# An adaLN block with a gated scan and a top-2 expert layer: GpSimd's row scatters spread over later turns

## What is computed

```python
x = L0_attn_x                                  # (32, 256, 128): 8192 tokens
h = layernorm(x) * (1 + ca) + sa               # ca, sa, ga, ... from silu(c) @ wmod
g = sigmoid(h @ Wg.T + bg); a = sigmoid(h @ Wd.T + bd); v = h @ Wv.T + bv
x = x + ga * (scan(h_t = a_t * h_{t-1} + (1 - a_t) * v_t) * g)
h = layernorm(x) * (1 + cb) + sb
probs = softmax(h @ gate_w.T + gate_b)         # 8 experts
topk_vals, topk_idx = top_k(probs, 2)
y_e = relu(h @ w1_e + b1_e) @ w2_e + b2_e      # hidden width 512
x = x + gb * sum over the two chosen experts of gate * y_e
```

## Time and profile before the change

| | |
|---|---|
| median of three executions | 471.75 us (471.03 to 472.77) |
| span of the profiled execution | 489.7 us |
| the same, over the median | 17.9 us |
| PE, DVE, ACT, POOL busy | 83%, 85%, 61%, 43% of the span |
| attention and routing, up to about | 213 us |
| FFN loop, from there on | 277 us |
| row scatters by GpSimd (L562) | 64, between 92.3 and 212.9 us |

### The profile page before, as it was taken

How to read it: one execution, slowest core, us unless ns; L and a number is a source line. 1 busy time by engine, 2 the same in 40 slices (tenths; PEclk the granted TensorE clock), 3 DMA queues, 4 the chain that set the end, 5 groups by cost and what they waited for, 6 DMA issues and landing times.

```text
span 489.7 us, 14521 instructions
## 1 busy us (share of the span) xinstructions
PE 407.1 (83%) x4122; PEld 337.3 (69%) x4123; DVE 417.7 (85%) x1159; ACT 297.8 (61%) x746; POOL 210.0 (43%) x225
## 2 busy tenths in 40 slices
PE   1959898877887472479999999999999999999960
PEld 1534546445555361359998999999999988998860
DVE  4989889949879759769999899999999999999980
ACT  1536888858787340156676676676676667666640
POOL 7023230683775554833333344444344333433451
PEclk9977889797889555599999999999999999999995
DMA  7624533452331332532333333333323332222220
GB/s 227 169 63 165 162 115 108 173 197 81 116 130 67 114 131 82 168 109 84 91 91 90 79 87 82 89 90 97 85 81 85 82 85 78 71 76 77 67 66 14
DMA packets 47259, 50.51 MB, mean 103 GB/s; under 512 B 5343, under 2 KB 40880, under 8 KB 47203
## 3 DMA queue, kind: packets, MB, share of 16 engines
q1 hardware_dynamic: 39152, 32.64, 24.3%
q0 software_dynamic: 6976, 16.93, 9.4%
q10 hardware_dynamic: 1074, 0.23, 0.2%
HBM read 26.90 MB, written 24.57 MB: 105 GB/s over the span
## 4 chain that ended last, share of the span: by engine, by line
PE 59%; DVE 11%; POOL 10%; issue 9%; SPq 5%; DMA 2%; ACT 2%; POOLq 0%; ACTq 0%; DVEq 0%
PE bank L1500 8%; PE bank L1498 8%; PE bank L1515 8%; PE bank L1518 8%; PE bank L1516 8%; PE bank L1499 8%; POOL sorted_rows L562 8%; PE bank L1364 4%; SPq L422 3%; PE bank L1510 2%; PE bank L1484 2%; DVE st L856 1%; POOL rstd L549 1%; PE bank L1370 1%; DMA xs<-in_L_attn_x_dram 1%
## 5 line engine op out<-in xcount | busy, mean ns | idle before, releaser
L588 POOL DMA_INDIRECT out_dram<-tg,midx x90 | 104.5, 1161 | 163.1 <-DVE tg L1293 149.0
L752 ACT ACTIVATE xs<-bank,b1col 128x256 f32<-128x256 f32 x360 | 136.6, 492 | 21.9 <-PE bank L1500 19.9
L1516 PE MATMUL bank<-w2hi,w2f 128*128 x720 | 119.0, 219 | 1.0 <-issue 1.0
L1515 PE MATMUL bank<-w2hi,xs 128*128 x720 | 119.2, 219 | 0.0
L1274 DVE TENSOR_TENSOR w2f<-xs 128x1024 f16<-128x1024 f32 x90 | 110.3, 1226 | 3.1
L1498 PE MATMUL bank<-xh,w1hi 128*128 128x256 f16 x360 | 99.4, 276 | 2.8 <-ACT xs L752 2.8
L1499 PE MATMUL bank<-xl,w1hi 128*128 128x256 f16 x360 | 99.2, 276 | 0.0
L1500 PE MATMUL bank<-xh,w1lo 128*128 128x256 f16 x360 | 99.2, 275 | 0.0
L1518 PE MATMUL bank<-w2lo,xs 128*128 x720 | 99.0, 219 | 0.0
L562 POOL DMA_INDIRECT sorted_rows<-pay,idx x64 | 68.0, 1062 | 42.8 <-DVE idx L1071 23.5
L1515 PEld LDWEIGHTS bank<-w2hi,xs 128*128 128x128 f16 x720 | 70.2, 98 | 1.8 <-issue 1.1
(11 more groups left out here) (232 smaller groups left out, 673.5 us busy)
## 6 DMA issues: line engine op xcount, KB each, us to landing
xs<-sorted_rows SPq DMA_DIRECT2D x45, 260.0 KB
sorted_rows<-padt SPq DMA_DIRECT2D x10, 582.0 KB
xs<-sorted_rows SPq DMA_DIRECT2D x45, 128.0 KB
w2f<-in_L_ffn_w_dram SPq DMA_DIRECT2D x4, 512.0 KB, 3.8
xs<-in_L_ffn_w_dram SPq DMA_DIRECT2D x4, 512.0 KB, 4.0
xs<-in_L_attn_x_dram SPq DMA_DIRECT2D x3, 512.0 KB, 8.8
out_dram<-tg,midx POOLq DMA_INDIRECT x90
sorted_rows<-pay,idx POOLq DMA_INDIRECT x64
```

What stands on the lines that cost most here:

```text
L588: pool.indirect_dma_start(out_rows, bass.IndirectOffsetOnAxis(midx[k][:, t:t + 1], 0), yout[k][:, t, :], None, bounds_check=TOK - 1, oob_i ...
L752: ins = act.activation(hf[e][:, cc, :], bank[2 * e + cc // 2][:, (cc % 2) * TW:(cc % 2 + 1) * TW], ACT.Relu, bias=b1col[:, bass.ds(ex[e] * ...
L1515: pe.matmul(o[t], hh[n % 2][e][:, cc, t * P:(t + 1) * P], whi, start=False, stop=False)
L1516: pe.matmul(o[t], hl[n % 2][e][:, cc, t * P:(t + 1) * P], whi, start=False, stop=False)
```

## The change

The table of turns is new, and GpSimd takes two new waits. In the turns 8 to 15 the group ahead of `scales` is scattered only once that same turn's scan on VectorE has made its `r` (the count of `r_ready` is the turn's number plus one), and what stands behind `scales` only once that turn's residual is written (`x1_ready`). `scatter` itself, its own waits and the last four groups are as before.

```diff
-SCATTER_IN = {7: ((), (0,)), 8: ((1, 2), ()), 10: ((3, 4), ()), 11: ((), (5,)), 12: ((6,), (7,)), 14: ((8, 9), ()),
-              15: ((10, 11), ())}
+SCATTER_IN = {8: ((0,), ()), 9: ((1,), ()), 10: ((2,), ()), 11: ((3,), ()), 12: ((4,), ()), 13: ((5,), (6,)),
+              14: ((7,), ()), 15: ((8,), (9, 10, 11))}
...
             for turn in range(NG):
                 before, behind = SCATTER_IN.get(turn, ((), ()))
+                if before:
+                    pool.wait_ge(r_ready, turn + 1)
                 for g in before:
                     scatter(g)
                 for n, (end, _, _) in enumerate(BATCHES):
                     if end == turn and n not in QUICK:
                         scales(n)
+                if behind:
+                    pool.wait_ge(x1_ready, turn + 1)
                 for g in behind:
                     scatter(g)
             pool.sem_inc(landed, 1)
```

## The result

The changed kernel takes 467.34 us (median of ten executions, 464.94 to 469.53), the kernel before, on the same chip, 470.84 us (ten executions, 468.02 to 472.77). The ratio is 0.993 with a 95% interval of 0.9902 to 0.9959: 0.7%, or 3.3 us, faster. The interval reaches to 0.9959, so that the change is faster is clear, but that it is faster by over 0.5% is not beyond doubt. The forecast was 470.9 us in a range of 464.5 to 475.5; the time lies inside, but on the side of rival A, which had 0.35, and not in "no difference", which had 0.42.

A forecast was written before the change was run, and what follows sets the result against it. The first 213 us, up to VectorE's table, were taken to decide. Five terms summed to -8.6 us in the profiled execution, but only -0.9 us was taken as likeliest for plain ones: 471.75 - 0.9 = 470.9 us, range 464.5 to 475.5.

The forecast's parts named there:

- rival A: Faster: the stalls beside scatter runs are real; 463.2 us in full, 467.5 us at half; chance 0.35.
- no difference: Whole kernel: time within about 0.5%, 2.4 us, of the kernel before; chance 0.42.
- The reading of the profile: Turns 9, 11 and 15: idles and late signals of up to 5.9 us follow GpSimd's long scatter runs.
- the likeliest case: Stalls belong to the profiled execution, so only -0.9 us remains: 470.9 us, own range 469.4 to 474.1; chance 0.42.
- if the FFN loop takes the same 277 us in both: FFN loop: if equal, plain executions have some 195 us ahead of it, the profiled one 213.
- The rule on records that hold back their producers: Trace block holds back producers rather than lose records, so stalls may come from recording; would leave -0.9 us.
- Terms 1, 2 and 4: Idles removed by splitting or moving scatter runs: turn 9, -4.6 us; turns 11 and 12, -1.6; turn 15, -6.1.
- Term 3: Turn 13: VectorE's 0.94 us wait for `scales`, which GpSimd does behind group 6, goes whatever becomes of the stalls: -0.9 us.
- Term 5: From turn 15's scan to the table: the price of the new long scatter run, +4.6 us, bounds 0 to 5.9.
- Rival B: Slower: only long runs hurt, and the change makes the longest before the table; +9.5 us, +4.7 at half; chance 0.23.
- The cover at the end: End of the loop: 14.6 us to spare between scatter landing and table shrinks to 5.4 or 1.8 us; costed at nothing.
- The last sixteen start 1.6 us late, which the FFN's first tiles cover: Start of the FFN: group 12's places come 19.2 us after the scan, GpSimd is free at 20.8; costed at nothing.

The follow-up runs named there:

- experiment 1: The kernel before, unchanged, timed and profiled once more: 470.66 us, ratio 1.0016.
- 9: The kernel before with group 6 behind the `scales` of turn 12 and group 7 behind those of turn 13, no new waits: 466.31 us, 0.9935.
- Experiment 10: The change's early table with the old end and no new waits, against the kernel before: 467.53 us, 0.9942.
- experiment 4: The kernel before with only turn 15 as in the change, groups 8 to 11 behind its scan, with the waits there: 469.73 us, 0.9998.
- experiment 8: The change itself once more, unaltered, against the kernel before on a second chip: 468.16 us, 0.993.
- experiment 11: The change itself a third time, unaltered, against the kernel before on a third chip: 467.03 us, 0.9945.
- 2: The change's new table of turns without its two new waits, against the kernel before: 468.49 us, 0.9952.
- 3: The change with its waits until turn 13, old order in turns 14 and 15, against the kernel before: 467.97 us, 0.9948.
- 5: The kernel before with the `scales` of turn 12 ahead of group 6: 469.22 us, 0.996.
- 6: The kernel before with groups 6 and 7 both ahead of the `scales` of turn 12: 475.32 us, 1.0097.
- 7: The change with groups 4, 5 and 6 all ahead of the `scales` of turn 12, against the kernel before: 474.28 us, 1.0078.

## Why the prediction was right, and where it was wrong

**The reading of the profile** is the step that failed: "Beside the ends of these runs the other engines stand still for no reason of their own", and "that is the pattern the change goes for". Three coincidences in one execution were taken for a pattern. The runs of scatters are in experiments 1 and 9 as well, and the engines do not stand still there. The prediction saw the warning, a span 17.9 us over the median of the plain executions, and drew the right conclusion for the likeliest case, that plain executions have no such stalls. But it named the recording as such as the cause, and that is not borne out: the twelve profiles taken after it, of changed and unchanged kernels, have spans of 464.9 to 474.7 us, and their own times lie in the range of the other executions of the same kernel, but for two that are 0.1 us above it (9 and 10) and one 0.9 us below (4); in experiment 1 it is 471.22, where the median is 470.66. The recording does not slow this kernel noticeably; that one execution was slow. What made it so stays open. It was slow in the FFN too: from the table to the last tile's `xl` (L1265) it took 266.2 us, experiment 1 took 260.7, so "if the FFN loop takes the same 277 us in both" does not hold, and 5.5 of the 20.3 us between the two spans lie there. The rule on records that hold back their producers (the Trainium skill, NOTIFIC — the notification-queue block, section Overflow) does not tell why one profile of the program stalls and the next does not.

**Terms 1, 2 and 4** (-4.6, -1.6, -6.1 us): nothing. The stalls that they remove are in no other profile. Experiment 4, which changes only turn 15, gives 0.9998.

**Term 3** (-0.9 us) is the mechanism, and the sum went wrong in its size. The wait is 2.91 us in experiment 1, where the earlier trace rows have 0.94. The stalls of the first profile may have hidden a part of it, but they are not needed for a short wait: experiment 4 has none of them and waits 0.98 us. What goes with the length of the wait is how early GpSimd starts the eight scatters of groups 5 and 6. Ahead of VectorE's scan of turn 13 (L928, L932 in experiment 4) they start by 5.2 us in the first profile (131.72; 136.93), by 4.5 in experiment 4 (122.06; 126.57) and by 2.8 in experiment 1 (125.43; 128.22). How often an execution of the kernel before has the short wait and how often the long one, no run shows, so the mean worth of term 3 is not known. A wait of 2.91 us gone would be 0.9938 of 470.84 us, one of 0.94 us 0.998. The measured 0.993 [0.9902, 0.9959] leaves out the second and not the first. The sum should have put this wait first, since it was the only idle in the rows whose releaser was named and whose queue order the edit changes.

**Term 5** (+4.6 us): nothing before the table. From the end of `r` in turn 15 (152.48) to the table (177.48, the row above plus its 0.28) it takes 25.0 us in the changed kernel with the long run, and 25.0 in experiment 1 with its own shorter ones (156.95 to 181.97). Rival B falls with it: the scatters beside VectorE's serial work cost it nothing.

**The cover at the end.** The landing of group 11 was never late: SP loaded the first tile at 179.43 us, right behind the table. "The last sixteen start 1.6 us late, which the FFN's first tiles cover" did not hold everywhere. The chain of waits of the changed kernel, at the start of the FFN:

```profile
199.63 1.67 POOL sorted_rows L562
...
201.61 3.54 DMA sorted_rows<-pay,idx
...
207.10 0.35 POOL out_dram L592
...
209.25 3.18 DMA out_dram<-tg,midx
...
213.98 0.43 DVE xl L1269
```

and the row of DVE that waits there:

```profile
212.46 0.16 DVE L1285 TENSOR_TENSOR midx<-xs,drop 128x2 int32<-128x2 int32 x1 [4.38 <-DMA out_dram<-tg,midx]
```

GpSimd's last row scatter starts at 201.61 us, 24.1 us behind the table, where in experiment 1 it starts at 198.7, 16.7 us behind a later table. The results of the first tiles queue up behind it, and VectorE waits for the buffer of their indices. From the table to the last tile's `xl` (L1269) it took 262.3 us here, where experiment 1 took 260.7; but with a wait of 1.05 us in experiment 8 it took 261.0, and 1.13 us in experiment 11 gave 260.5. Experiment 4, which has the same end, waits 1.16 us at L1285 and took 260.9. So the late end costs 1.6 us in one execution of four and at most 0.3 in the other three. Experiment 10, which has the old end, is no faster than the change beside it (0.9942 and 0.9945). A cost in every execution is not shown.

**The forecast.** That the time fell inside the range is in part luck: the range took in the likeliest case and rival A, and the measured 467.34 us is nearly rival A's 467.5 "at half", although neither its stalls nor its price exist in the other profiles. The rank of the cases was right in kind: the big stalls did not belong to the plain executions, and what was left was term 3. It was wrong in the step from there to "no difference", since 0.9 us is under the 2.4 us that can be told, and what the change brought, 3.3 us, is over it.

## What to carry to other kernels

When a profile's span lies several per cent over the plain times, take another profile before any idle is priced; here one repetition would have struck out four of five terms and tripled the fifth. To size a term, one repetition is not enough either: the same wait is 0.94, 2.91 and 0.98 us in three executions of the old order. On a queue that both produces a small result for another engine and issues long series of DMAs, put the small result first: eight scatters of 1.27 us ahead of 1.7 us of `scales` were the loss, and moving two groups behind them repaired it. Compare profiles over the stretch from the last common point, not by the place in the span.

## What the runs showed that was not expected

One program gave two profiles 20.3 us apart (489.7 and 469.4 us), and in the longer one signals of PE reached the waiting engine up to 5.9 us late.

The granted clock of PE moves between executions of one program, in stretches that no edit touches. Busy time by stretch (span; PE, PEld, DVE, ACT, POOL busy; clock; DMA share; GB/s), first the changed kernel, then experiment 8, the same program:

```profile
90.00:150.00 60.00, 52.66 (x290) 35.12 (x290) 53.66 (x243) 49.12 (x108) 41.06 (x43) 0.85 0.35 129
```

```profile
90.00:150.00 60.00, 47.85 (x297) 32.49 (x296) 54.88 (x249) 51.52 (x113) 42.17 (x44) 0.95 0.37 137
```

At 0.95 PE is busy for 4.8 us less in the 60 us, with seven more instructions; such differences are larger than the term that decided the case.

The mean granted clock of whole executions shows that a part of the gain goes with the clock. None of 108 executions of the kernel before (experiments 1 to 11) is over 0.927. Of the 34 of the change (result, 8 and 11), 15 are at 0.929 to 0.934, with a median of 465.8 us. Every kernel without the wait in turn 13 has such executions (also 2, 3, 5, 9 and 10), and none of those with it has (1, 4, 6 and 7). At a like clock the change is less far ahead: at 0.922 to 0.923 its median is 468.2 us (4 executions) against 469.5 (22), at 0.908 to 0.909 it is 470.2 (6) against 471.0 (13). So the edit moves time and clock together, and how much of the 3.3 us is the wait itself and how much comes with the clock is not settled.

The row scatters were not slowed by a busy VectorE: the twenty from 152.76 on start every (177.42 - 152.76) / 19 = 1.30 us, while VectorE is busy for 23.5 of these 24.7 us. Those beside the FFN's first loads take longer: from 182.02 to 201.61 one starts every 19.59 / 11 = 1.78 us, and the one at 177.42 took 4.30 us. What lengthens them was not tried.
